# Turning quantised activations in f32, the gate's product in PSUM, and the layer norm of tiles 4 to 7 on VectorE alone

## The reference

```
x = x + mixer(ctx, layernorm(x))      # a selective state-space scan
x = x + ffn(layernorm(x))

mixer:  xin = ctx @ in_proj.T ; u = silu(conv4(xin) + conv_b)        # 256 channels
        dt_low, B, C = split(x_proj @ u)                             # 8, 16, 16
        dt = softplus(dt_proj @ dt_low + dt_b) ; A = -exp(A_log)
        state = state * exp(dt * A) + (dt * u) * B                   # 16 states a channel, 256 steps
        y = sum_n(state * C) + D * u ; out = (y * silu(z)).T         # z = layernorm(x)

ffn:    h = gelu(silu(bitlinear(x, w1, b1)))                         # 256 -> 1024
        h = layer_norm(h) * g + b
        out = bitlinear(h, w2, b2)                                   # 1024 -> 256
bitlinear: rms-norm a row, round it to whole numbers in +-127 by its largest value,
           multiply with weights rounded to -1, 0, 1, scale back, add the bias
```

## Time and profile before

| | |
|---|---|
| median of three runs | 211.79 us (210.87 to 212.91) |
| the profiled execution | 211.12 us; its span, first to last instruction, 209.3 us |
| VectorE busy | 173.8 us (83%) |
| TensorE matmuls | 162.5 us (78%); weight loads 118.5 us |
| ScalarE | 162.5 us (78%) |
| GpSimd | 148.5 us (71%) |
| mean granted clock of TensorE | 0.878 of 2.4 GHz |

### The profile page before, as it was taken

One profiled execution on the slowest core, in us unless ns is written; L12 is line 12 of the kernel. 1 busy time (PEld: TensorE's weight loads), 2 busy tenths in 40 slices (PEclk: granted clock), 3 DMA queues, 4 the chain that ended last, 5 costly groups with the idle time before them and its releaser, 6 DMA issues. The chain is left out here.

```text
span 209.3 us, 3383 instructions
## 1 busy us (share of the span) xinstructions
PE 162.5 (78%) x1158; PEld 118.5 (57%) x1158; DVE 173.8 (83%) x267; ACT 162.5 (78%) x262; POOL 148.5 (71%) x142
## 2 busy tenths in 40 slices
...
GB/s 176 277 57 354 403 324 0 2 3 190 160 57 0 0 3 124 176 106 2 0 2 0 139 165 99 5 0 0 0 3 0 25 0 2 0 25 27 30 25 75
DMA packets 7137, 15.89 MB, mean 76 GB/s; under 512 B 904, under 2 KB 4432, under 8 KB 6992
## 3 DMA queue, kind: packets, MB, share of 16 engines
...
## 5 line engine op out<-in xcount | busy, mean ns | idle before, releaser
L793 POOL TENSOR_TENSOR st<-st,bc 128x1024 f32<-128x1024 f32 x32 | 76.1, 2393 | 19.9 <-DVE st L949 19.6
L949 DVE TENSOR_TENSOR_SCAN st<-dA,ps 128x1024 f32<-128x1024 f32 x32 | 71.9, 2273 | 2.1 <-PE ps L481 2.1
L481 PE MATMUL ps<-diagB,dtuT 64*128 64x128 f32 x512 | 47.0, 311 | 7.7 <-DVE st L949 6.3
L645 ACT ACTIVATE dA<-dt,negA 128x255 f32<-128x255 f32 x128 | 52.4, 494 | 0.1
L481 PEld LDWEIGHTS ps<-diagB,dtuT 64*128 64x128 f32 x512 | 35.6, 200 | 20.4 <-issue 8.7
L518 PE MATMUL ps<-id_f,st 128*128 128x128 f32 x256 | 35.8, 287 | 1.6 <-POOL st L793 1.6
L518 PEld LDWEIGHTS ps<-id_f,st 128*128 128x128 f32 x256 | 30.1, 148 | 4.3 <-POOL st L793 2.0
L558 PE MATMUL ps<-rows_sb,diag 128*128 128x512 f32 x32 | 17.4, 672 | 3.0 <-ACT w_raw L678 3.0
L576 PE MATMUL ps<-w2q,q2T 128*128 128x256 bf16 x64 | 11.8, 347 | 5.8 <-DVE res L1073 3.0
L1023 DVE BATCH_NORM_STATS2 stats<-w_raw 128x6 f32<-128x512 f32 x16 | 10.2, 678 | 5.0 <-ACT w_raw L682 5.0
L829 POOL TENSOR_TENSOR w_raw<-w_raw,rows_sb 128x1024 f32<-128x1024 f32 x6 | 14.1, 2354 | 0.0
...
## 6 DMA issues: line engine op xcount, KB each, us to landing
...
w_raw<-w2T SPq DMA_DIRECT2D x1, 1024.0 KB, 11.0
...
```

The lines of the kernel that those rows point to most:

```text
L481: mm = nc.tensor.matmul(o[:, i:i + SG // 2, t, r, :], dtuT[rows, b % 2, h, t, :], diagB[rows, b % 2, t, n, :], start=True, stop=True)
L645: e = nc.scalar.activation(dA[:, k % DA_RING, i * L + 1:(i + 1) * L], dt[:, h, b % 2, 1:L], ACT.Exp, scale=negA[:, h, n:n + 1])
L793: tt(s, s, bc[:, ng].rearrange("p s l -> p (s l)"), ALU.mult).then_inc(prod_done, 1)
L949: nc.vector.tensor_tensor_scan(st[:, k % ST_RING, :], dA[:, k % DA_RING, :], slot(k), 0.0, ALU.mult, ALU.add).then_inc(scanned, 1)
```

## The change

It has four parts.

- **q1 and q2 are turned in f32.** The scaled value with ROUND in it (xc, or hid) goes to TensorE as it is, turned against the f32 identity; ScalarE's copy out of PSUM takes ROUND off and makes it bf16. The casts L1012, L858 and L1064, the buffers q1 and q2 and the bf16 identity go. A turned q2 fills both banks of `big` instead of one. A slot of hid is free once its tile is turned (`q2_turned`), not once it is cast.
- **The gate's product is written back into yT** in PSUM instead of the buffer yg, and x1 reads it there. TensorE may start the next batch's sums in yT when x1 has read it (`x1_half`), not when the gate has (`gate_step`).
- **LAST is 4:** VectorE applies the layer norm of tiles 4 to 7; ScalarE's norm and GpSimd's shift are left for tiles 0 to 3.
- **All four tables are new.**

```diff
-                        pe.wait_ge(gate_step, TPB * b)
+                        pe.wait_ge(x1_half, TPB * b)
...
-                        mm = nc.tensor.transpose(tq1[:, o:o + P], q1[:, t, h * P:(h + 1) * P], id_b[:, :])
+                        mm = nc.tensor.transpose(head[:, o:o + P], xc[:, t, h * P:(h + 1) * P], id_f[:, :])
...
-                pe.wait_ge(*q2_of(t))
+                pe.wait_ge(w_done, t + 1)
                 for k in range(KB):
-                    mm = nc.tensor.transpose(tq2[:, k * P:(k + 1) * P], q2[:, t % 2, k * P:(k + 1) * P], id_b[:, :])
+                    mm = nc.tensor.transpose(big[:, k * P:(k + 1) * P], hid[:, t % HSLOTS, k * P:(k + 1) * P], id_f[:, :])
...
-                nc.scalar.activation(q1T[:, :, :, :].rearrange("p t h n -> p (t h n)"), tq1[:, 0:TPB * HALVES * P],
-                                     ACT.Copy).then_inc(q1T_done, 1)
+                nc.scalar.activation(q1T[:, :, :, :].rearrange("p t h n -> p (t h n)"), head, ACT.Identity,
+                                     bias=-ROUND).then_inc(q1T_done, 1)
...
-                    act.wait_ge(q2_done, t - HSLOTS + 1)
+                    act.wait_ge(q2_turned, t - HSLOTS + 1)
...
-                nc.scalar.activation(q2T[:, t % 2].rearrange("p k n -> p (k n)"), tq2, ACT.Copy).then_inc(q2T_done, 1)
+                nc.scalar.activation(q2T[:, t % 2].rearrange("p k n -> p (k n)"), big, ACT.Identity, bias=-ROUND).then_inc(q2T_done, 1)
...
-        LAST = TILES - TPB
+        LAST = 4
...
-                if i >= TPB:
-                    dve.wait_ge(x1_half, i - TPB + 1)
-                tt(yg[:, t, :], yT[:, t, :], siluzT[:, b, t, :], ALU.mult).then_inc(gate_step, 1)
+                tt(yT[:, t, :], yT[:, t, :], siluzT[:, b, t, :], ALU.mult).then_inc(gate_step, 1)
...
-                tt(x_nat[:, t, b, :], x_nat[:, t, b, :], yg[:, t, :], ALU.add).then_inc(x1_half, 1)
+                tt(x_nat[:, t, b, :], x_nat[:, t, b, :], yT[:, t, :], ALU.add).then_inc(x1_half, 1)
...
-                ts(q1[:, :, :], xc[:, :, :], ROUND, None, ALU.subtract).then_inc(q1_done, 1)
...
-                ts(q2[:, t % 2, :], hid[:, t % HSLOTS], 1.0, -ROUND, ALU.mult, ALU.add).then_inc(q2_done, 1)
...
-    "scale_b:11 convolve:3 scale_rest:11 xdbl:3 scale_b:12 b_cols:2",
+    "b_cols:2 scale_b:11 scale_b:12 scale_rest:11",
```

More of the change, by code:

```diff
@@ L68 @@
     "",
[6 rows of a table removed]
+    "wmean:0",
+    "",
+    "dt_neg:2",
+    "gate:0 gate:1 spread_b:8 x1:0 spread_b:9 x1:1",
+    "dt_mask:2 clip_weights:0 dt_sum:2 ln1:0 spread_b:10 spread_b:11",
+    "",
+    "clip_weights:1",
+    "dt_neg:3 quant1:0",
+    "",
+    "spread_b:12 spread_b:13 spread_b:14",
     "spread_b:15",
[6 rows of a table removed]
+    "gate:2 gate:3 x1:2 bn2:0 x1:3 dt_mask:3 dt_sum:3 gain:0",
+    "ln1:1",
+    "",
+    "bn2:1",
     "",
[1 row of a table removed]
+    "quant1:1",
     "",
[3 rows of a table removed]
+    "gate:4 gain:1 gate:5",
+    "amax2:0 x1:4 scales2:0 x1:5",
+    "",
+    "amax2:1 bn2:2 ln1:2 scales2:1 gain:2",
+    "bn2:3 amax2:2 quant1:2 scales2:2 res:0",
+    "gain:3",
+    "res:1 bn2:4 gate:6 gate:7 x1:6 amax2:3 x1:7 scales2:3 ln1:3 res:2 quant1:3 gain:4 bn2:5 amax2:4 "
+    "gain:5 bn2:6 amax2:5 scales2:4 gain:6 bn2:7 scales2:5 gain:7 amax2:6 res:3 scales2:6 amax2:7 "
+    "scales2:7 res:4 res:5 res:6 res:7",
 )
 SCALAR_AT = (
[7 rows of a table removed]
[20 rows of a table added]
     "",
@@ L143 @@
     "",
-    "dt_series:3",
+    "",
+    "root2a:0 shift:0 root1:1",
     "",
     "",
-    "root2a:0",
+    "",
     "root2a:1",
-    "shift:0",
-    "root1:1",
-    "root2b:0 out_scale:0",
+    "",
+    "root2b:0",
     "shift:1",
     "",
-    "root2b:1 root1:2 quant2:0",
-    "out_scale:1 root2a:2",
-    "",
-    "",
[L158 to L161, removed]
@@ L162 @@
-    "out_scale:5 add_b2:2 root2b:7 add_b2:3 out_scale:6 out_scale:7",
+    "",
+    "root2a:2 root2b:1 root1:2 shift:2 out_scale:0 out_scale:1 root2b:2 root2a:3",
+    "out_scale:2",
+    "",
+    "shift:3 add_b2:1 root2b:3 root1:3 root2a:4 out_scale:3 root2a:5 root2b:4 add_b2:2 root2a:6 "
+    "out_scale:4 root2b:5 root2a:7 root2b:6 out_scale:5 root2b:7 out_scale:6 add_b2:3 out_scale:7",
 )
 PE_AT = (
-    "scale_b:1 xdbl:1 scale_rest:1 dtraw:1 scale_b:2 scale_rest:2 turn_half:1",
-    "convolve:2 scale_b:3 wsum:0 scale_rest:3 turn_z:0 scale_b:4",
@@ L193 @@
-    "scale_rest:31",
-    "turn_q2:0",
-    "",
-    "mm2:0 turn_q2:1",
-    "turn_q1:3 mm1:6 mm1:7 mm2:1 turn_q2:2 mm2:2 turn_q2:3 mm2:3 turn_q2:4 mm2:4 turn_q2:5 turn_q2:6 "
-    "mm2:5 turn_q2:7 mm2:6 mm2:7",
+    "xdbl:1 scale_b:1 scale_rest:1 turn_half:1 dtraw:1 scale_b:2 scale_rest:2",
+    "scale_b:3 b_cols:1 scale_rest:3 convolve:2 scale_b:4 scale_b:5 scale_rest:4 xdbl:2",
+    "scale_rest:5",
+    "",
+    "scale_b:6 turn_du:1 scale_rest:6 scale_b:7 scale_rest:7",
+    "scale_b:8 wsum:0 scale_rest:8 scale_b:9",
@@ new lines @@
+    "scale_rest:9 dtraw:2 scale_b:10",
+    "scale_rest:10 turn_z:0",
+    "b_cols:2 scale_b:11 scale_b:12 scale_rest:11",
+    "scale_rest:12",
+    "convolve:3",
+    "scale_b:13 scale_rest:13 xdbl:3 turn_du:2",
+    "scale_b:14 dtraw:3 scale_b:15 scale_rest:14 turn_z:1 scale_rest:15",
+    "scale_b:16 scale_rest:16 turn_q1:0 mm1:0 scale_b:17 b_cols:3 scale_rest:17",
+    "",
+    "scale_b:18 scale_rest:18",
+    "mm1:1 scale_b:19 scale_rest:19",
+    "turn_du:3 scale_b:20 turn_z:2 scale_rest:20 scale_b:21 turn_z:3",
```

98 lines of the change are left out of this document (40 added, 58 removed), and 74 rows, old and new, of tables (SCALAR_AT, VECTOR_AT).

## The result

| | before | after |
|---|---|---|
| median of the runs | 212.35 us (4 runs, 210.87 to 213.57) | 204.97 us (4 runs, 203.05 to 205.08) |
| span of the profiled run | 209.3 us | 203.3 us |
| GpSimd busy | 148.5 us | 136.3 us |
| mean granted clock | 0.878 | 0.947 |

The ratio is 0.9736, with a 95% interval of 0.9687 to 0.9784: 2.6% faster. It is taken from the fast executions of both kernels, and so is not the quotient of the two medians (0.965). 207.6 us was predicted, with 202.5 to 212.5 as the range. Of the 6.0 us of span the stage up to the scaling of tiles 6 and 7 gave 1.5, the hand-over nothing, and the last stretch 4.6. The forecast had 2.6, 0 and 1.6: the sum holds because two sizes erred in opposite directions. The 1.5 of the first stage, moreover, is no gain of the change, as the part on the prediction shows: the profile of the kernel before has a stretch at a low clock there.

The account below looks back on a forecast made before the run. VectorE was taken to bound the kernel up to 170.1 us, then an engine relay with GpSimd late. -2.6 + 0 - 1.6 = -4.2 gave span 205.1, plus 1.8 and 0.7: 207.6 us, range 202.5 to 212.5.

Parts of the forecast that it names:

- Stage A: First scan to the mark (scaling of tiles 6 and 7 ends): less VectorE work, -2.6 us, mark at 167.5 us.
- The 10.4 us of gaps: VectorE's idle time from first scan to the mark: kept at 10.4 us, 3 us each way, with +0.2 taken.
- Hand-over: From scaling of tiles 6 and 7 to silu of tile 6, 6.5 us: slow mm1 of tile 6 again, 0 change.
- The low end: Between scaling of tiles 6 and 7 and silu of tile 6: at best -2.6 us.
- Stage B: Silu of tile 6 to the end, 32.7 us: ScalarE's work falls, its waits stay, -1.6 us.
- The second count: ScalarE's last stretch, from its last-but-one exps: 56.5 us work plus 13.9 waits, last copy at 199.2, span 203.4 us.
- the first count: Whole span divided at two marks, the changes of its three stretches summed: -4.2 us, span 205.1 us.
- Rival 1: Last stretch: with GpSimd early, half the waits and the slow mm1 go, about 203.0 us; chance 0.17.
- Rival 2: Up to the mark: xdbl 3 waits for the shared head bank, TensorE idles, gaps take the gain, 211.8 us; chance 0.20.
- Rival 3: x1 adds: not cheaper, as VectorE writes PSUM slower or still waits, +2.2, 209.8 us; chance 0.05.
- Rival 4: ScalarE's table loads: each switch costs 1.38 us more than its row, 212.8 us; chance 0.01.
- Rival 5: Tiles 2 to 7 at the end: TensorE falls to 1.2 GHz, mm1 costs 5.6 instead of 3.0, 217 us; chance 0.12.

Follow-up runs that it names:

- Kernel 2: LAST = 4 alone on the kernel before, so VectorE also applies the layer norm of tiles 4 and 5: ratio 0.995 to the kernel before.
- kernels 6 and 7: Changed kernel with the layer norm of tiles 4 and 5 back on three engines, 0.991; changed kernel plus four unused f32 matmuls on TensorE, 0.957 (to before).
- kernel 9: Kernel before, product still in SBUF, with both x1 adds right behind their batch's gates for batches 0 to 2: ratio 1.034 to the kernel before.

## Why the prediction was right, and where it was not

**Stage A, -2.6 predicted, -1.5 measured (-2.1 from the first scan, which began 0.6 us later).** The mechanism of this term, less work for VectorE and with it an earlier mark, failed, and that its size is near is luck. Two things went wrong.

The first is the base. The profile of before has TensorE at 0.57 from 77.50 to 85.40 us, and three scans waited 2.1 us for their fills there. Kernel 2, the same program as before up to the mark, kept its clock in its profiled execution. Its windows from the first scan to the mark and over that stretch:

```profile
26.16:168.16 142.00, 115.70 (x965) 87.55 (x962) 134.60 (x182) 121.44 (x211) 115.57 (x88) 0.96 0.17 60
77.50:85.40 7.90, 7.58 (x76) 6.07 (x78) 7.90 (x5) 7.09 (x16) 7.79 (x4) 1.00 0.36 128
```

and the changed kernel, first scan to mark:

```profile
26.13:168.65 142.52, 120.37 (x1000) 92.69 (x1000) 134.22 (x181) 126.47 (x217) 114.13 (x89) 0.99 0.17 61
```

So with the clock up in both, stage A takes 142.5 us with the change (141.7 and 142.6 in kernels 6 and 7, the same order) and 142.0 without it: no gain can be seen. The 10.4 us of gaps that the prediction kept held waits that another execution of the same program does not have. Whether the new order makes such a stretch rarer is open; the five other kernels with it had 0.91 to 1.00 between 75 and 100 us, before 0.86. The ratio of 0.974 is of several executions of each kernel and does not hang on this; the split of the 6.0 us is of two profiles only.

The second is VectorE's work. The adds came as priced: 5.4 to 3.2 us. The casts went. But the work did not fall by 2.8: 134.22 us against 134.60 in kernel 2. Other passes with two SBUF inputs got longer. VectorE by shape, each kernel in the stretch to 170 us, before:

```profile
L891 DVE SCALAR_TENSOR_TENSOR sp_e<-sp_v 128x512 f32<-128x512 f32 x3 | 2.6, 862 | 0.0
...
L907 DVE COPY_PREDICATED sp_ln<-sp_mask,sp_ser 128x512 f32<-128x512 int32 x3 | 2.2, 739 | 0.0
```

and after:

```profile
L891 DVE COPY_PREDICATED sp_ln<-sp_mask,sp_ser 128x512 f32<-128x512 int32 x3 | 3.5, 1169 | 0.0
L875 DVE SCALAR_TENSOR_TENSOR sp_e<-sp_v 128x512 f32<-128x512 f32 x3 | 3.3, 1096 | 0.0
```

These two alone take back 2.0 of the 3.5 us of adds and casts; 1.3 of it, the COPY_PREDICATED, belongs to the new order, since the other pass took 3.2 in kernel 2 as well. Two of the six executions are the cause: VectorE's timeline of the changed kernel, and GpSimd's,

```profile
39.37 2.02 DVE L891 COPY_PREDICATED sp_ln<-sp_mask,sp_ser 128x512 f32<-128x512 int32 x1
...
81.83 1.67 DVE L875 SCALAR_TENSOR_TENSOR sp_e<-sp_v 128x512 f32<-128x512 f32 x1
```

```profile
35.98 4.79 POOL L783 TENSOR_TENSOR st<-st,bc 128x1024 f32<-128x1024 f32 x2
...
80.59 2.36 POOL L783 TENSOR_TENSOR st<-st,bc 128x1024 f32<-128x1024 f32 x1
```

They end 0.6 us behind GpSimd's products (41.39 against 40.77, 83.50 against 82.95), about their own length, like the adds of kernel 9. Before, the first of them began at 37.97 and took 0.75, with GpSimd idle. The prediction looked for this effect among the adds and the passes of the last stage alone. The gaps are 8.3 us against 7.4 in kernel 2. The wait for the weights' mean is gone, as laid out by hand; the 3.5 us behind a convolve did not come; the one for gelu of tile 4 did, and one for mm2 that was not foreseen:

```profile
DVE res L1048 <- PE ps L566: 2.5, 1, 2.5
DVE stats L1003 <- ACT w_raw L672: 2.2, 1, 2.2
```

**Hand-over, 0 predicted, 6.53 for 6.46 measured.** Right, and for the reason given: mm1 of tile 6 ran at 1.2 GHz again. The low end, -2.6 with mm1 of tile 6 at 2.4 GHz, is what the four unused matmuls then gave (3.9 us, so -2.6).

**Stage B, -1.6 predicted, -4.6 measured.** This step was mis-sized as well. ScalarE's work fell by 2.3, near the 1.6; its waits fell by 2.3 as well (9.85 to 7.54 us), and I had kept them, with the sentence that f32 turning gives back what the missing q2 cast saves. The runs show otherwise. The changed kernel and its four variants that keep q2 in f32 have 28.1 to 28.3 us there, whatever their product, layer norm or clock; the one with casts has 33.8, and the kernels of the old order 32.1 to 34.8. Of the four late f32 turns the first took 1.94 us, the second 1.62 and the last two 1.09, so the 1 us more per tile that was booked came once and a half; the cast costs its 1.04 and the wait for GpSimd's queue, together 5.2 us for tile 4 where I had placed it. Whether the order or the missing cast gives more of it stays open, as the old order can't hold the f32 turns without moving them: a slot is free only when it is turned, mm1 of tile 5 needs silu of tile 4 done, and stands ahead of the turn of tile 0 that would free its slot. And what is late next is not ScalarE, as the prediction says: in the last stretch the chain has 9.1 us of GpSimd and 4.3 of ScalarE, and from 179.8 to 189.4 us it is nearly all GpSimd's one-column steps. The sign "with ScalarE, not GpSimd, in the chain" did not come.

**Small prices.** A VectorE write to PSUM took 0.413 us, predicted 0.41. The copy of two f32 banks took 1.010, not the 1.12 that I took from silu. The second count had ScalarE's last copy end at 199.2, and it ended at 199.17, by luck, since its errors cancel: it starts 1.8 us earlier than thought (127.0 for 128.8), has 1.0 us less work (55.55 for 56.5) and 2.8 us more waits (16.65 for 13.9). Its span, 203.4, was right to 0.1; I had put it second because the first count has the later mark.

**The rivals.** Rival 1 (ScalarE runs through, 203.0) is nearer to the median of 205.0 than the forecast is, but its conditions came by half: ScalarE still waited 7.54 us in the last stretch, and mm1 of tile 6 stayed slow. Rival 2 says that gaps take the gain of stage A. They did take part of it, but not in the place it named: the clock stayed up, and xdbl 3 waited 1.33 us:

```profile
72.73 1.04 PE L421 MATMUL ps<-cv,xproj_sb 128*24 128x256 f32 x4 [1.33 <-DVE diagB L918]
```

Rival 3 did not come: the adds took 0.40. Rival 4: the load at 126.80 us is followed by silu at 128.09, 1.29 us later:

```profile
126.80 1.28 ACT L668 ACT_TABLE_LOAD   x1
128.09 1.12 ACT L668 ACTIVATE w_raw<-ps,sm 128x1024 f32<-128x1024 f32 x1
```

The Trainium skill (ScalarE: Activation LUTs, What ACT_TABLE_LOAD costs) adds a drain of about 1.38 us; the trace does not show it. Rival 5 did not come: the bias products of tiles 3, 4, 5 and 7 took 1.88 to 1.96 us. Its sum was off by one: 10.4 on -4.2 gives 218 and not 217.
